# Transposing the next block's normalised rows with VectorE and on-chip transfers instead of TensorE

## What is computed

```python
x = x + xattn(layernorm(x), ctx)      # q = xn@Wq+bq; softmax(q k^T/sqrt(32)) v; relu(.@W1+b1)@W2+b2
xn = layernorm(x)
top1 = argmax(xn @ Wg.T)
x = x + sum_e (top1 == e) * (gelu((xhat*s_e + b_e) @ w1_e + bb1_e) @ w2_e + bb2_e)
```

## Time and profile before

| | us |
|---|---|
| median of 3 runs | 1405.73 (1405.03 to 1407.58) |
| profiled execution | 1402.3 |
| its span, first to last instruction | 1400.3 |
| TensorE busy | 1382.0 (99%) |
| VectorE busy | 991.0 (71%) |
| ScalarE busy | 612.0 (44%) |
| GpSimd busy | 334.0 (24%) |

### The profile page before, as it was taken

One profiled execution on the slowest core, in us unless ns is written; L12 is line 12 of the kernel. 1 busy time (PEld: TensorE's weight loads), 2 busy tenths in 40 slices (PEclk: granted clock), 3 DMA queues, 4 the chain that ended last, 5 costly groups with the idle time before them and its releaser, 6 DMA issues.

```text
span 1400.3 us, 23958 instructions
## 1 busy us (share of the span) xinstructions
PE 1382.0 (99%) x8590; PEld 1039.6 (74%) x8590; DVE 991.0 (71%) x2073; ACT 612.0 (44%) x1146; POOL 334.0 (24%) x293
## 2 busy tenths in 40 slices
PE   8999999999999999999999999999999999999998
PEld 5486868677776868686867777686868686788897
DVE  6667676686767676777767676767676766649887
ACT  4534334443424343534434342524243343448886
POOL 2311212021111212121201111121212120108887
PEclk9999999999999999999999999999999999999999
DMA  7200302021120303130212102020202021458885
GB/s 293 75 30 1 91 1 77 31 88 46 40 89 24 104 3 99 36 98 31 84 46 68 61 31 84 6 91 1 91 1 91 1 61 61 158 182 266 295 261 178
DMA packets 56916, 118.16 MB, mean 84 GB/s; under 512 B 8329, under 2 KB 16786, under 8 KB 55906
## 3 DMA queue, kind: packets, MB, share of 16 engines
q1 hardware_dynamic: 46002, 82.93, 19.2%
q0 software_dynamic: 10800, 33.70, 6.3%
HBM read 73.77 MB, written 44.66 MB: 85 GB/s over the span
## 4 chain that ended last, share of the span: by engine, by line
PE 96%; DVE 2%; issue 1%; POOL 1%; DMA 0%; ACT 0%; POOLq 0%; SPq 0%; DVEq 0%; ACTq 0%
PE bank L1176 25%; PE bank L1220 13%; PE bank L1200 12%; PE bank L1011 12%; PE bank L1099 8%; PE bank L1081 5%; PE bank L1601 4%; PE bank L1639 3%; PE bank L1036 3%; PE bank L1262 2%; PE bank L979 2%; PE bank L1585 2%; PE bank L1280 1%; PE bank L1055 1%; PE bank L883 1%
## 5 line engine op out<-in xcount | busy, mean ns | idle before, releaser
L1176 PE MATMUL bank<-actA,w 128*128 128x512 f32 x1536 | 368.8, 395 | 1.4 <-DVE actA L1147 1.4
L1176 PEld LDWEIGHTS bank<-actA,w 128*128 128x128 f32 x1536 | 282.4, 188 | 63.5 <-issue 5.6
L1089 ACT ACTIVATE E<-bank 77x512 f32<-77x512 f32 x256 | 132.3, 591 | 170.1 <-PE bank L1081 170.1
L1220 PE MATMUL bank<-w,actH 128*128 128x512 f32 x768 | 195.6, 400 | 0.0
L1200 PE MATMUL bank<-w,actH 128*128 128x512 f32 x768 | 184.8, 393 | 0.0
L1011 PE MATMUL bank<-actA,wq 128*128 128x512 f32 x768 | 182.7, 390 | 0.0
L1049 DVE TENSOR_REDUCE mx<-bank 128x4 f32<-128x308 f32 x256 | 104.6, 472 | 101.1 <-PE bank L1036 101.1
L1220 PEld LDWEIGHTS bank<-w,actH 128*128 128x128 f32 x768 | 138.6, 188 | 44.5 <-issue 18.3
L1011 PEld LDWEIGHTS bank<-actA,wq 128*128 128x128 f32 x768 | 142.7, 188 | 28.2 <-issue 0.5
L1200 PEld LDWEIGHTS bank<-w,actH 128*128 128x128 f32 x768 | 142.0, 188 | 28.2
L1185 ACT ACTIVATE actH<-bank,b 128x512 fp32r<-128x512 f32 x128 | 88.2, 689 | 161.8 <-PE bank L1176 160.2
(11 more groups left out here) (179 smaller groups left out, 1911.1 us busy)
## 6 DMA issues: line engine op xcount, KB each, us to landing
rowB<-region SPq DMA_DIRECT2D x71, 258.0 KB, 3.8
xn<-in_x SPq DMA_DIRECT2D x64, 256.0 KB, 2.8
rows<-in_x SPq DMA_DIRECT2D x64, 256.0 KB, 3.3
w_raw<-in_W SPq DMA_DIRECT2D x2, 2048.0 KB, 11.8
e_raw<-in_E SPq DMA_DIRECT2D x16, 256.0 KB, 2.8
region<-padrow SPq DMA_DIRECT2D x9, 258.0 KB, 4.2
e_parts<-e_high SPq DMA_DIRECT2D x8, 256.0 KB, 2.0
e_parts<-e_low SPq DMA_DIRECT2D x8, 256.0 KB, 2.3
```

The source lines that it names most:

```text
L1089: act.activation(E[0:M, g % 2, h, :], of("ST", b, g, h)[0:M, :], ACT.Exp).then_inc(S["act_exp"], 1)
L1176: mm = pe.matmul(p[:], w, a, start=k == 0 and j == 0, stop=k == KD - 1 and j == 2)
L1220: mm = pe.matmul(p[:], actH[:, ha, m, P * s:P * s + P], w2[:, hw, m, :], start=n == 0, stop=n == 23)
```

## The change

From the second block on, the transposes leave TensorE. The chain of XSTAT gets four more VectorE instructions: each transposes one tile of `xn` in place, in blocks of 32 by 32. What is left is to move block (t, f) of the 4 by 4 blocks of each 128x128 chunk to the place of block (f, t), across partitions. The new step XTD does that with transfers on SyncE's queue from SBUF to SBUF, 16 for each pair of tiles, 32 for a block of tokens, each of 32 partitions times 8 pieces of 32 numbers. They write to `xT_raw`, in the memory of the low half of `actQ`, free once the scores of the block before have been made. The new step XTS is the old split with `xT_raw` as its source instead of a PSUM bank.

In blocks 3 to 10 and in block 0, XTD stands behind the DRAIN that closes the hidden layer. In blocks 1, 2 and 11 to 14 ("early") XSTAT moves to the start of the hidden layer, XTD stands behind the DRAIN at m = 3, and X2STAT(b-1) moves from the start of the hidden layer to behind XTD. XNLOAD moves ahead in the list. In blocks 3 to 10 the drips from m = 4 on are 8 instead of 6.

```diff
-    xn = [sb(f"xn{i}", [P, D]) for i in range(SUB)]
+    xn_all, xn_at = sb("xn", [P, SUB, D])
+    xn = [xn_all[:, i, :] for i in range(SUB)]
+    xT_raw = at("xT_raw", [P, SUB, KD, P], F32, actQ_at + 4 * KD * BLK)
...
+            early = b > 0 and prep is None and not last or None
             if prep is not None:
                 step("E1_ACC", prep)
+            elif early:
+                step("XSTAT", b + 1)
+                step("DRIP", 8)
             elif b:
                 step("X2STAT", b - 1)
                 step("DRIP", 8)
...
-                    step("DRIP", 6)
+                    step("DRIP", 6 if prep is None or m < 4 else 8)
...
+                if early and m == 3:
+                    for i in range(2):
+                        step("XTD", b + 1, i)
+                    step("X2STAT", b - 1)
...
-                if m == (3 if prep is None else 4) and not last:
+                if m == (3 if prep is None else 4) and not last and not early:
                     step("XSTAT", b + 1)
...
                 step("DRAIN")
+                if early is None:
+                    for i in range(2):
+                        step("XTD", b + 1, i)
                 step("YA", b, 0)
...
-                    step("XT", b + 1, s)
+                    step("XTS", b + 1, s)
...
+                if b:
+                    for s in range(SUB):
+                        dve.wait_ge(S["dve_xn"], SUB * b + s + 1)
+                        dve.transpose(xn[s][:], xn[s][:]).then_inc(S["dve_xnT"], 1)
+                        yield
...
+        HB = HD
+        XTD = 16 * (P // HD) ** 2
+        def sp_xtd(sp, b, i):
+            sp.wait_ge(S["pe_s"], KD * b)
+            sp.wait_ge(S["dve_xnT"], SUB * (b - 1) + 2 * i + 2)
+            for t in range(P // HB):
+                for f in range(P // HB):
+                    src = xn_all[HB * t:HB * t + HB, 2 * i:2 * i + 2, :].rearrange("p s (k f j) -> p (s k) f j", k=KD, j=HB)
+                    to = xT_raw[HB * f:HB * f + HB, 2 * i:2 * i + 2].rearrange("p s k (t j) -> p (s k) t j", j=HB)
+                    sp.dma_start(to[:, :, t], src[:, :, f]).then_inc(ld_xT[i], 16)
+        def act_xts(act, b, s):
+            act.wait_ge(ld_xT[s // 2], XTD * b)
+            act.wait_ge(S["pe_h"], MF * b)
+            act.activation(actA[:, 0, :, P * s:P * s + P], xT_raw[:, s], ACT.Identity
+                           ).then_inc(S["act_xT"], 1)
+        def dve_xts(dve, b, s):
+            if s == 0:
+                drain()
+            dve.wait_ge(S["act_xT"], SUB * b + s + 1)
+            dve.tensor_tensor(actA[:, 1, :, P * s:P * s + P], xT_raw[:, s],
+                              f32(actA[:, 0, :, P * s:P * s + P]), ALU.subtract).then_inc(S["dve_xT"], 1)
```

More of the change, by code:

```diff
@@ L108, in xattn_moe_kernel @@
     csb, _ = sb("csb", [P, BLK])
-    xn = [sb(f"xn{i}", [P, D]) for i in range(SUB)]
-    xn_at = xn[0][1]
-    xn = [t[0] for t in xn]
+    xn_all, xn_at = sb("xn", [P, SUB, D])
+    xn = [xn_all[:, i, :] for i in range(SUB)]
     b2bc, _ = sb("b2bc", [P, D])
@@ L240, in xattn_moe_kernel @@
         ld_x = [[sem(f"ld_x{i}_{s}") for s in range(SUB)] for i in range(2)]
+        ld_xT = [sem(f"ld_xT{i}") for i in range(SUB // 2)]
         st_v, ld_v = sem("st_v"), sem("ld_v")
@@ L250, in xattn_moe_kernel @@
             "act_wq dve_wq act_w1 pool_w1 act_w2 dve_w2 act_kbd dve_sel dve_tri "
-            "dve_xn pool_xb pe_xT act_xT dve_xT pe_q act_q dve_q pe_sm dve_max pe_mt act_mt pe_s act_exp "
+            "dve_xn dve_xnT pool_xb pe_xT act_xT dve_xT pe_q act_q dve_q pe_sm dve_max pe_mt act_mt pe_s act_exp "
             "pe_sums dve_rc pe_av dve_n act_o pool_o dve_o pe_h act_h dve_h pe_y dve_x2 dve_row pool_ones pe_gate dve_gate "
@@ L386, in xattn_moe_kernel @@
             step("HK", b, 3)
+            prep = b - 1 - PREP0 if PREP0 < b <= PREP0 + NE else None
             if last:
@@ L389, in xattn_moe_kernel @@
                 step("EB_LOAD")
-            prep = b - 1 - PREP0 if PREP0 < b <= PREP0 + NE else None
+            else:
+                step("XNLOAD", b + 1, 0)
+                if prep is None:
+                    step("XNLOAD", b + 1, 2)
+            early = b > 0 and prep is None and not last or None
             if prep is not None:
                 step("E1_ACC", prep)
+            elif early:
+                step("XSTAT", b + 1)
+                step("DRIP", 8)
             elif b:
@@ L420, in xattn_moe_kernel @@
                 if m:
-                    step("DRIP", 6)
-                if not last and m == 0:
-                    step("XNLOAD", b + 1, 0)
-                if not last and m == 0 and prep is None:
-                    step("XNLOAD", b + 1, 2)
+                    step("DRIP", 6 if prep is None or m < 4 else 8)
                 if context is not None and m == 0:
@@ L690, in flat, with xn_left @@
             return ap.rearrange("p k n -> p (k n)")
+        def xn_left(sp, b, s):
+            if b:
+                sp.wait_ge(ld_xT[s // 2], XTD * b)
+            else:
+                sp.wait_ge(S["pe_xT"], s + 1)
         def sp_xnload(sp, b, s0):
@@ L694, in sp_xnload @@
                 if b:
-                    sp.wait_ge(S["pe_xT"], SUB * (b - 1) + s + 1)
+                    xn_left(sp, b - 1, s)
                 if b == 1:
@@ L721, in sp_e1raw @@
         def sp_e1raw(sp, e):
-            sp.wait_ge(S["pe_xT"], SUB * (PREP0 + e + 2))
+            for s in range(SUB):
+                xn_left(sp, PREP0 + e + 1, s)
             sp.dma_start(e1_raw[:], A["E1"][:, :, e, :]).then_inc(L["e1raw"], 16)
@@ L756, in sp_tabload @@
         def sp_tabload(sp):
-            sp.wait_ge(S["pe_xT"], SUB * NBLK)
+            for s in range(SUB):
+                xn_left(sp, NBLK - 1, s)
             sp.dma_start(jt[:], A["jt"][:, 0:N1, :]).then_inc(L["jt"], 16)
@@ L1718, in xattn_moe_kernel @@
             "XT": {"pe": pe_xT, "act": act_xT, "dve": dve_xT},
+            "XTD": {"sp": sp_xtd},
+            "XTS": {"act": act_xts, "dve": dve_xts},
             "XB": {"pool": pool_xb},
```

## The result

The changed kernel took **1633.02 us** (median of 4 runs, 1630.14 to 1633.68) against 1406.49 us for the kernel before on the same chip: a ratio of **1.161** (95% interval 1.159 to 1.163). The profiled execution took 1632.48 us with a span of 1630.7; before it was 1402.3 and 1400.3. So 230 us have to be found between the two traces.

The account below looks back on a forecast made before the run. TensorE, busy 1382.0 of 1400.3 us, was taken to bound the kernel; 111.2 (blocks 3 to 10) + 14.3 (block 0) + 2.2 (early blocks) = 127.7 us gave 1533 us, range 1485 to 1680.

Parts of the forecast that it names:

- The issue: SyncE's queue: 32 transfers a block, 0.45 us from one to the next, 14.0 us from first issue to last.
- The upper bound, 0.74: SyncE's queue: 0.74 us from one issue to the next, from a load issued when the queues were full; 1676 us.
- 8.9 us a block at the lower bound: Blocks 3 to 10: added time with issues every 0.37 us and no clock price; 1488 us in all.
- Removed: TensorE: 15 of 16 blocks lose the transposes of normalised rows, 1.74 us each, 26.1 us together.
- start: Blocks 3 to 10: first transfer issued at 466.2, once VectorE's two transposes and SyncE's row loads are through.
- landing: Transfers: 2.0 us from an issue to its landing in SBUF, with 3.8 us as the upper end.
- splits: From the second group's landing to the first Q product: two ScalarE passes and the last VectorE subtraction, 2.2 us.
- The clock: TensorE behind the idle in blocks 0 and 3 to 10: a lower granted clock adds 2.5 us a block.
- The early blocks: Blocks 1, 2, 11 to 14: transfers hidden behind a 2.1 us rank-product wait; net +0.4 us each, 2.2 together.
- its upper case: All changed blocks: issues every 0.74 us with the clock price; early blocks +10.8 each, sum 270, 1676 us.
- Small pieces that cost double: Transfer engines: a 128-byte write costs two 512-byte packets, 0.84 us a transfer, engines set the pace; 1736 us, chance 0.13.
- Not slower: Blocks 3 to 10: transfers all over by 471.3, issues under 0.03 us apart; 1393 us; chance 0.02 faster, 0.01 neutral.

Follow-up runs that it names:

- the kernel with 85 matmuls: Changed kernel plus 85 filler matmuls on TensorE ahead of the first Q product in blocks 0 and 3 to 10; 1621.67 us, ratio 1.156.
- the kernel where none met GpSimd's additions: Against the kernel before: new route in six early blocks only, 16 merged issues, six on ScalarE's queue, one-hot ahead of the transposes; 1395.5 us, ratio 0.992.

## Why the prediction was right, and where its terms were off

The direction and the mechanism were right: TensorE waits at Q in nine blocks for transfers whose pace the issue sets, and it is granted a lower clock behind the wait. The time, 1633, lies inside the range but 100 us above the forecast. About 48 of these 100 come from the nine late blocks and 51 from the six early ones, where the mechanism too was partly wrong. By its steps:

- **The issue, the mis-sized term.** The prediction took 0.45 us from one to the next, by counting runs between two rows of loads of 0.33 and 0.57 us. It was 0.655 (0.611 and the gap). 31 x 0.205 = 6.4 us a late block, 57 us over nine, and in early blocks the same 6.4 us broke the cover. The step that failed is the interpolation by runs: merged transfers with 512 pieces and flat ones with 32 rows both cost about what 256 pieces did. The upper bound, 0.74, held. (The prediction's 8.9 us a block at the lower bound is 8.8 by its own numbers; that changes nothing.)
- **Removed, start, landing, splits.** Q's start in block 5 can be followed: transposes in 2.48 us for the predicted 2.5, the first issue 5.86 us after TensorE's start on the second layer (441.47 to 447.33) for the predicted 6.0 (460.20 in the timeline before, to 466.2), landing 1.93 for 2.0, splits and start 2.1 for 2.2. All these terms stood; only VectorE alone set the first issue, since the row loads were through at 446.47. From the first issue to Q lie 24.4 us for 18.2, and the difference is the issue's alone.
- **The clock.** Predicted 2.5 us a late block, measured 1.8 in block 5 (7.27 against 5.44) and 1.7 to 2.2 in the nine. The source of the 2.5 does not carry it: the matmuls at the start of the program are slow, but the view gives their granted clock as 1.00 (the row below), so they show no price of a lower clock, and it was luck that the number came near. The row for the last 10 us shows a lower clock and no price. Also, the forecast gave the early blocks no price for the clock, and there it was paid twice: behind a pause of 1.73 us (7.32 for 5.72) and behind 3.88 (8.62 for 5.60). The extra of the hidden layer over the whole program, 375.3 - 368.8 = 6.5 us, is four times 1.6, for the four of six blocks in which the short pause was followed by slow matmuls.
- **The early blocks.** Predicted +0.4 each, measured +8.9 (the run with early blocks alone). The pause at the rank product came as foreseen, 1.73 us for 2.1. That the transfers would be hidden behind it was the wrong half: it was a margin of 0.9 us (1156.6 against 1157.5), and 6.4 us of issuing were missing. Early blocks that idle at Q were one of the prediction's own signs of being wrong, and its upper case had them late (+10.8).
- **Rivals.** Small pieces that cost double: refuted. In the 18 us from 448 to 466 the queue moved 7402 packets with 31.5% of 16 engines, 12.3 ns a packet (the row below), or 0.20 us per transfer, against 0.84 in that rival and 0.42 in the forecast. The Trainium skill ("DMA: Bandwidth & Descriptors", Why small descriptors are slow) spares transfers within SBUF from the penalty on small pieces; the trace agrees in that a small packet is not dearer than a large one: 12.3 ns for 128 B here, 26 ns for the 512 B of the earlier trace rows. By the byte it is about twice as dear, and the rows compare two kinds of transfer. "Not slower" needed issues under 0.03 us and was never near; it came true only by changing where the route is used.

The transfers of the changed kernel from 448 to 466 us (queue: packets, MB, share of 16 engines), and the start of the program in the kernel before (TensorE's busy us and count, granted clock, share of the transfer engines, GB/s):

```profile
q1 hardware_dynamic: 7402, 0.97, 31.5%
```

```profile
6.80:9.00 2.20, 2.19 (x5) 1.00 1.09 404
```

By blocks: 111.2 predicted for blocks 3 to 10 with block 0's 14.3 make 125.5, measured 173; the early ones 2.2, measured 53.3.

## What to carry to other kernels

Count the issues of a transfer route first: here one issue between SBUF tiles cost 0.59 to 0.63 us of its queue for 256 pieces, 512 pieces or 32 rows, so fewer and larger ones, spread over two queues, were worth far more than what the transfers carry. A route that takes load off the busiest engine pays only in the stages where its whole length, issue and landing and what stands behind, fits behind other work; use it there and keep the old one elsewhere. A margin of a microsecond is none, since a pause can cost twice: the wait, and the clock behind it.

## What the runs showed of the hardware that was not expected

- An issue of a transfer from SBUF to SBUF over 32 partitions took 0.61 us with 256 pieces of 128 B, 0.63 with 512 pieces, 0.59 with 32 rows of 2 KB; a row load of 128 rows of 2 KB from HBM took 0.33 in the same program when nothing held it.
- While two queues (SyncE's, ScalarE's) issued at once, each kept its pace: 16 in 10.56 us beside 15 in 10.06.
- ScalarE's issues lay beside its own passes: one at 1134.32 for 0.59 us while a bias step ran from 1134.21 to 1134.90.
- A VectorE transpose of 128x512 f32 in blocks of 32x32 took 0.67 us, 0.62 from one to the next.
- TensorE's granted clock was 0.50 at first behind pauses of 3.45, 3.88 and 19.18 us, and the shorter pause could cost more: behind 19.18 us it was 0.51 from 471.7 to 475.0 and then 1.00 (Q 1.8 us slower), behind 3.88 us it was still 0.50 from 1217 to 1219, then 0.98 (Q 3.0 us slower).
- Behind a pause of 1.73 us the next 24 matmuls took 7.3 us in four early blocks of the changed kernel and 5.7 in two; with two queues it was six and none, with the early blocks alone three and three. In the kernel with 85 matmuls a pause of 1.74 us was followed by Q in 5.74 us. Whether a short pause costs anything is not decided by its length alone; what decides it is not shown.
- The same subtraction took 0.68 us in the kernel where none met GpSimd's additions, and 1.22 in the median, up to 1.76, where they ran beside them.
